# Attention scores and row maxima regrouped: 4 heads x 32 queries per matmul, keys in steps of 32

## The reference

```python
q = x @ wq_w.T + wq_b                    # x: (2, 1024, 256); 16 query heads of 16, 4 key heads of 16
k = x @ wk_w.T + wk_b
v = x @ wv_w.T + wv_b
q = _rope(q); k = _rope(k)               # the angle depends on the head alone
k = jnp.repeat(k, G, axis=1)             # G = 4 query heads share a key head
v = jnp.repeat(v, G, axis=1)
att = jnp.einsum('bhqd,bhkd->bhqk', q, k) / HD ** 0.5
att = jnp.where(mask[None, None], att, -jnp.inf)      # causal
att = jax.nn.softmax(att, axis=-1)
y = jnp.einsum('bhqk,bhkd->bhqd', att, v)
x = _layernorm(x + y @ cp_w.T + cp_b)
# then a feed-forward layer: one shared and 16 routed experts, 4 per token, and a second layernorm
```

## Time and profile before

| | |
|---|---|
| median of 3 runs | 551.21 us |
| span of the profiled execution, first to last instruction | 548.3 us |
| PE / DVE / ACT / POOL busy | 525.8 / 435.9 / 372.3 / 290.6 us |
| granted TensorE clock | 0.998 of full speed over the span |

### The profile page before, as it was taken

One profiled execution on the slowest core, in us unless ns is written; L12 is line 12 of the kernel. 1 busy time (PEld: TensorE's weight loads), 2 busy tenths in 40 slices (PEclk: granted clock), 3 DMA queues, 4 the chain that ended last, 5 costly groups with the idle time before them and its releaser, 6 DMA issues.

```text
span 548.3 us, 12215 instructions
## 1 busy us (share of the span) xinstructions
PE 525.8 (96%) x3796; PEld 359.4 (66%) x3796; DVE 435.9 (79%) x1126; ACT 372.3 (68%) x841; POOL 290.6 (53%) x336
## 2 busy tenths in 40 slices
PE   8999999999999899989999898899999999999885
PEld 4656444444554454534433387799999999999874
DVE  2388989899889899999992177987878788787685
ACT  2444777787888688968879566366766667667534
POOL 5121232555412777267978856477644454545292
PEclk9999999999999999999999999999999999999999
DMA  5934174400523811321042352378544443341495
GB/s 150 179 66 65 31 191 145 82 8 21 91 62 88 207 58 46 82 81 51 32 128 82 104 178 66 112 227 262 159 139 128 130 118 111 111 133 46 160 414 194
DMA packets 53710, 64.96 MB, mean 118 GB/s; under 512 B 8091, under 2 KB 47406, under 8 KB 53648
## 3 DMA queue, kind: packets, MB, share of 16 engines
q1 hardware_dynamic: 45968, 46.45, 31.4%
q0 software_dynamic: 7056, 17.60, 9.2%
q10 hardware_dynamic: 624, 0.13, 0.1%
HBM read 32.49 MB, written 25.62 MB: 106 GB/s over the span
## 4 chain that ended last, share of the span: by engine, by line
PE 75%; DVE 10%; POOL 6%; issue 3%; ACT 2%; DMA 2%; SPq 1%; POOLq 0%; DVEq 0%; ACTq 0%
PE psH L1705 13%; PE psS L1506 12%; PE psO L1491 11%; PE psT L1476 10%; PE psS L1568 4%; PE psX L1673 3%; PE psG L1716 3%; PE psS L1511 2%; PE psS L1592 2%; POOL xs_scratch L766 2%; PE psY L1733 2%; PE psY L1730 2%; PE psY L1729 2%; PE psY L1732 2%; PE psY L1731 2%
## 5 line engine op out<-in xcount | busy, mean ns | idle before, releaser
L885 ACT ACTIVATE prob<-psT 128x512 f32<-128x512 f32 (+3 forms) x384 | 167.3, 495 | 51.6 <-PE psT L1476 49.0
L1161 DVE TENSOR_REDUCE MX<-psS 128x1 f32<-128x512 f32 (+3 forms) x344 | 182.6, 595 | 9.1 <-PE psS L1511 3.9
L1506 PE MATMUL psS<-KS,QS 96*128 96x512 bf16 (+3 forms) x384 | 109.9, 328 | 4.4 <-DVE MX L1161 2.5
L839 POOL DMA_INDIRECT y_scratch<-ys,dst x79 | 76.9, 973 | 65.7 <-ACT ys L1040 50.8
L1476 PE MATMUL psT<-QS,KS 98*128 98x512 bf16 (+3 forms) x384 | 107.0, 328 | 0.9 <-ACT prob L885 0.4
L795 POOL TENSOR_SCALAR_AFFINE_SELECT prob<-prob 128x512 f32<-128x512 f32 x64 | 42.4, 665 | 91.8 <-ACT prob L885 91.6
L1491 PE MATMUL psO<-prob,V 128*32 128x512 f32 (+3 forms) x768 | 81.3, 498 | 1.2 <-POOL prob L795 1.2
L1705 PE MATMUL psH<-wU,xh 128*128 (+1 forms) x380 | 80.8, 334 | 0.5 <-DVE z L1313 0.4
L766 POOL DMA_INDIRECT xs_scratch<-x1row,slotu x64 | 65.4, 1022 | 26.9 <-issue 16.2
L1476 PEld LDWEIGHTS psT<-QS,KS 98*128 98x128 bf16 x384 | 33.7, 97 | 52.9 <-ACT prob L885 34.6
L1506 PEld LDWEIGHTS psS<-KS,QS 96*128 96x128 bf16 x384 | 37.1, 98 | 45.4 <-DVE MX L1161 22.5
(11 more groups left out here) (260 smaller groups left out, 1003.0 us busy)
## 6 DMA issues: line engine op xcount, KB each, us to landing
xs<-xs_scratch SPq DMA_DIRECT2D x80, 134.0 KB
y<-y_scratch SPq DMA_DIRECT2D x16, 512.0 KB, 10.2
QS<-qp SPq DMA_DIRECT2D x48, 128.0 KB, 4.5
wU_raw<-in_L_ffn_w_routed_dram SPq DMA_DIRECT2D x32, 176.0 KB, 2.9
xs_scratch<-padrow SPq DMA_DIRECT2D x1, 2144.0 KB
xs_scratch<-padrow SPq DMA_DIRECT2D x16, 134.0 KB
x1row<-in_L_attn_x_dram SPq DMA_DIRECT2D x4, 512.0 KB, 5.8
out_dram<-x1row SPq DMA_DIRECT2D x7, 256.0 KB, 2.6
```

The source lines that it names most:

```text
L839: nc.gpsimd.indirect_dma_start(y4_dram, bass.IndirectOffsetOnAxis(ap=dst[:, n % NSEL, t:t + 1], axis=0), ys[:, n % NYS, t, :], None, bound ...
L885: nc.scalar.activation(prob[:, step % NPROB, h, 0:HALF - c0], ps[:, 0:HALF - c0], ACT.Exp).then_inc(s_Tfree, 1)
L1161: found = nc.vector.tensor_reduce(out=MX[:, c0 // HALF, heads[0]:heads[-1] + 1, i - TH * q], in_=src, op=ALU.max, axis=AX_X)
L1506: last = mm(ps[:, e * dist:e * dist + cols], QS[0:ROWS, QAT[(k // 2) % NSLOT], g % 2 * G + h, (i - TH * q) * P:(i - TH * q + 1) * P], KS[b ...
```

## The change

The queries of a half are regrouped. The half's 512 queries are 16 blocks of 32; block p holds queries 32p to 32p+31. The columns of QS are written in a new order, query 32p + i in column 16 i + p, by reading the projection's input with a step of 32 columns. From this follow:

- `smax`: one matmul takes 4 heads x 32 queries of one block, whose columns lie 16 apart, as its 128 stationary columns. A block needs keys only up to its own end, (p+1) x 32 of the half. Two blocks with together 512 keys share a PSUM bank and one mask matmul, whose stationary matrix `spread_b` repeats a 32-row identity for the 4 heads; the mask has 32 columns per block. A q = 0 headgroup has 9 units with 16 score matmuls, 9 masks and 16 reduces, a q = 1 headgroup 16 more units of 512 keys.
- `mrow`: DVE's result, 128 partitions (4 heads x 32) by 16 blocks, already has the column order of QS, so SP sends it directly by two DMAs, each of 128 pieces of 16 bf16. Transpose and copy are gone, and M2 has two buffers.
- `st`: one matmul takes 4 heads x 128 queries (4 neighbouring columns, then 16 on), always 512 columns: 4, 3, 2 and 1 items on the diagonal. ACT's exponential writes 4 heads x 128. POOL clears the diagonal of the first chunk of a step and waits for that chunk alone; its pattern now steps through 4 blocks of 32.
- `evac` puts the queries back in order while it copies: it reads psO with a step of 4.
- ORDER is written anew (911 items for 1079), and the order of two projection splits is exchanged.

```diff
 def max_units(q):
-    if q:
-        return [(i, (h,), c, HALF, c0) for i in range(TH, TT) for h in range(G) for c0, c in ((0, HALF), (HALF, (i + 1) * P - HALF))]
-    units = [(0, (0, 1, 2, 3), P, P, 0)] + [(1, (h, h + 1), 2 * P, 2 * P, 0) for h in (0, 2)]
-    units += [(i, (h,), (i + 1) * P, HALF, 0) for i in (2, 3) for h in range(G)]
-    return units
+    near = [(NBLK - 1,)] + [(NBLK - 2 - i, i) for i in range(NBLK // 2 - 1)] + [(NBLK // 2 - 1,)]
+    return ([("far", p) for p in range(NBLK)] if q else []) + [("near",) + u for u in near]
+def segments(unit):
+    kind, *blocks = unit
+    if kind == "far":
+        return [(blocks[0], 0, HALF)]
+    return [(p, 0 if n == 0 else HALF - (p + 1) * QB, (p + 1) * QB) for n, p in enumerate(blocks)]
...
 ORDER = """
-aaaaaaaadadpaaldppdlpdaaaapalaaaaapaapamalpppaxxaaaxxaaxaalxxxaaxxvamaxxavxxxaaaxavaxaxpaxmaxaxaaxxaaxvxaaaxxaexpavmaaxx
+aaaaaaaadpdlaadapppldalaaaaaaaamaappaapapapxapaxdxwaxpaxaaxxaaavvaaxaamxlawxxpaxdaxvvxxaaalaexaxxvvxamaxxaxaaxvwvweaxaax
...
+        def heads_of(k, r0, r1):
+            g = HEADGROUPS[k][2]
+            return QS[r0:r1, QAT[(k // 2) % NSLOT], g % 2 * G:(g % 2 + 1) * G, :]
...
-                    sp.wait_ge(s_Tfree, T_NO[item])
-                    sp.dma_start(QS[ROWS:QROWS, QAT[(k // 2) % NSLOT], g % 2 * G:(g % 2 + 1) * G, :]
-                                 .rearrange("s h (i t) -> s (h i) t", t=P), MT[:, :]).then_inc(s_mrow, 16)
+                    sp.wait_ge(s_Sfree, S_NO[last_max(k)])
+                    for s in range(MROWS):
+                        sp.dma_start(heads_of(k, ROWS + s, ROWS + s + 1).rearrange("a h (i p) -> a (h i) p", p=NBLK),
+                                     M2[:, k % 2, s, :]).then_inc(s_mrow[k % 2], 16)
...
-                                            pattern=[[0, G], [1, P]], channel_multiplier=-1).then_inc(s_diag, 1)
+                                            pattern=[[0, G], [1, QB], [QB, G]], channel_multiplier=-1).then_inc(s_diag, 1)
...
-                    nc.scalar.activation(prob[:, step % NPROB, h, 0:HALF - c0], ps[:, 0:HALF - c0], ACT.Exp).then_inc(s_Tfree, 1)
+                    nc.scalar.activation(prob[:, step % NPROB, :, c * P:(c + 1) * P], ps.rearrange("p (h t) -> p h t", h=G),
+                                         ACT.Exp).then_inc(s_Tfree, 1)
...
-                    nc.scalar.copy(O[:, k % 2, :], psO[:, :]).then_inc(s_evac, 1)
+                    nc.scalar.copy(O[:, k % 2, :].rearrange("d (c p i) -> d c p i", c=TH, i=QB),
+                                   psO[:, :].rearrange("d (c i p) -> d c p i", c=TH, i=QB)).then_inc(s_evac, 1)
...
-                    found = nc.vector.tensor_reduce(out=MX[:, c0 // HALF, heads[0]:heads[-1] + 1, i - TH * q], in_=src,
-                                                    op=ALU.max, axis=AX_X)
+                    for p, at, cols in segments(unit):
+                        found = nc.vector.tensor_reduce(out=MX[:, int(q and unit[0] == "near"), p:p + 1], in_=ps[:, at:at + cols],
+                                                        op=ALU.max, axis=AX_X)
...
-                    mm(ps[:, 0:HALF - c0], KS[b][:, g, j * P:(j + 1) * P],
-                       QS[:, QAT[(k // 2) % NSLOT], g % 2 * G + h, c0:HALF], start=True, stop=True).then_inc(s_T, 1)
+                    mm(ps, KS[b][:, g, j * P:(j + 1) * P],
+                       heads_of(k, 0, QROWS).rearrange("r h (i p) -> r h i p", p=NBLK)[:, :, :, p1:p1 + P // QB],
+                       start=True, stop=True).then_inc(s_T, 1)
...
-                    for e, h in enumerate(heads):
-                        last = mm(ps[:, e * dist:e * dist + cols],
-                                  QS[0:ROWS, QAT[(k // 2) % NSLOT], g % 2 * G + h, (i - TH * q) * P:(i - TH * q + 1) * P],
-                                  KS[b][0:ROWS, g, c0:c0 + cols], start=True, stop=not masked)
-                        if masked:
-                            d = e * dist + cols - P
-                            last = mm(ps[:, d:d + P], ident_b[:, :], mask_b[:, :], start=False, stop=True)
+                    for p, at, cols in parts:
+                        last = mm(ps[:, at:at + cols], heads_of(k, 0, ROWS).rearrange("r h (i p) -> r (h i) p", p=NBLK)[:, :, p],
+                                  KS[b][0:ROWS, g, k0:k0 + cols], start=(at == 0), stop=not near)
+                    if near:
+                        d = [at + cols - QB for _, at, cols in parts]
+                        step = d[-1] - d[0]
...
+                        last = mm(to, spread_b[:, :], by, start=False, stop=True)
...
-                elif kind == "mrow":
-                    pe.wait_ge(s_Sfree, S_NO[last_max(item[1])])
-                    nc.tensor.transpose(ps[0:MROWS * G * TH, :].bitcast(BF16)[:, 0:P], M2[:, :, :].rearrange("p s r -> p (s r)"),
-                                        ident_b[:, :]).then_inc(s_T, 1)
...
-                        last = mm(ps[0:rows, 0:HALF], wT[:, k, :],
-                                  xT[:, k, half * HALF:(half + 1) * HALF], start=(k == 0), stop=(k == KC - 1))
+                        src = xT[:, k, half * HALF:(half + 1) * HALF]
+                        if m:
+                            src = src.rearrange("c (p i) -> c i p", i=QB)
+                        last = mm(ps[0:rows, 0:HALF], wT[:, k, :], src, start=(k == 0), stop=(k == KC - 1))
```

More of the change, by code:

```diff
@@ L45 @@
 NPROB = 3
+QB = P // G
+NBLK = HALF // QB
 assert NHALF * NKV == TT
@@ L173, in plan @@
         "v": [("pv", k, n) for k, n in STEPS], "n": [("norm", k) for k in range(NK)], "r": [],
-        "p": later_items(0) + first_items(1) + later_items(1), "x": [("st", k, n, h) for k, n in STEPS for h in range(G)],
+        "p": later_items(0) + first_items(1) + later_items(1), "x": [("st", k, n, c) for k, n in STEPS for c in range(chunks(k, n))],
         "w": [], "s": [], "o": [], "c": []}
@@ L184, in plan @@
             streams["c"] += [("scat", b, q, n) for n in range(TH * TOPK)]
-    streams["d"] = [("split",) + i[1:] for i in streams["a"] + streams["p"] if i[0] == "proj"]
+    projected = [i for i in streams["a"] + streams["p"] if i[0] == "proj"]
+    projected[2:4] = projected[3:1:-1]
+    streams["d"] = [("split",) + i[1:] for i in projected]
     for u, _ in weight_units():
@@ L189, in plan @@
         streams["o"] += [("wlow",) + u] if u[0] == "wB" else []
-    queues = {c: iter(items) for c, items in streams.items()}
+    return streams
+def plan():
+    queues = {c: iter(items) for c, items in item_streams().items()}
     return [next(queues[c]) for c in "".join(ORDER.split())]
@@ L234 @@
 SEL_NO = {item: n + 1 for n, item in enumerate(
-    i for i in SEQ if i[0] == "st" and i[3] == G - 1 and exp_steps(HEADGROUPS[i[1]][1])[i[2]][2])}
+    i for i in SEQ if i[0] == "st" and i[3] == 0 and exp_steps(HEADGROUPS[i[1]][1])[i[2]][2])}
 LASTCP = ("cp", B - 1, TT - 1)
@@ L443, in attention_moe @@
         s_qload = [sem(f"s_qload{i}") for i in range(NSLOT)]
-        s_mrow = sem("s_mrow")
+        s_mrow = [sem(f"s_mrow{i}") for i in range(2)]
         s_res = sem("s_res")
@@ L634, in run @@
                         last = 2 * (s - NSLOT) + 1
-                        sp.wait_ge(s_T, T_NO[("st", last, len(exp_steps(HEADGROUPS[last][1])) - 1, G - 1)])
+                        sp.wait_ge(s_T, T_NO[last_exp(last)])
                     if s:
@@ L725, in link @@
                 pool.wait_ge(s_pool, chain[0])
-            for m in (ident, ident_b, mask_b, padrow):
+            for m in (ident, ident_b, spread_b, mask_b, padrow):
                 nc.gpsimd.memset(m[:, :], 0.0).then_inc(s_const, 1)
@@ L1484, in run @@
                         pe.wait_ge(s_evac, k)
-                    st = ("st", k, n, G - 1)
                     if diag:
-                        pe.wait_ge(s_diag, SEL_NO[st])
-                    else:
-                        pe.wait_ge(s_Tfree, T_NO[st])
+                        pe.wait_ge(s_diag, SEL_NO[("st", k, n, 0)])
+                    if not diag or chunks(k, n) > 1:
+                        pe.wait_ge(s_Tfree, T_NO[("st", k, n, chunks(k, n) - 1)])
                     for h in range(G):
@@ L1503, in run @@
                         pe.wait_ge(s_qload[s % NSLOT], 16 * len(PAIRS) * (s // NSLOT + 1))
[L1504 to L1511 removed]
+                    near = unit[0] == "near"
+                    k0 = HALF if q and near else 0
+                    parts = segments(unit)
+                    for p, at, cols in parts:
[4 more added lines that the diff above has]
+                        step = d[-1] - d[0]
+                        to = ps[:, d[0]:d[0] + QB]
+                        if step:
+                            to = bass.AP(tensor=to.tensor, offset=to.offset, ap=[to.ap[0], (step, 2), (1, QB)])
+                        by = mask_b[:, :].unsqueeze(1).to_broadcast([P, 2, QB]) if step else mask_b[:, :]
+                        last = mm(to, spread_b[:, :], by, start=False, stop=True)
                     last.then_inc(s_S, 1)
```

79 lines of the change are left out of this document (38 added, 41 removed).

## The result

The changed kernel takes 584.62 us (median of 4 runs, 584.04 to 585.33) where the kernel before, on the same chip, takes 551.98 (four runs, 550.10 to 556.87): a ratio of 1.056, 95% interval 1.051 to 1.061. It is slower by 32.6 us; 538 was forecast, and the range ended at 556.

What follows compares the result with a forecast made beforehand. PE sets the pace with DVE close behind; -15.3 (DVE) + 0.3 + 0.6 (end) + 1 (selects) + 0.5 (evacuation) = -12.9 us takes the span from 548.3 to 535.4, so about 538 us measured; forecast 531 to 546, 8-in-10 range 528 to 556.

Steps and rivals of the forecast that it cites:

- POOL's select: Select in runs of 4 queries: 0.61 us as now, up to 0.5 more by an iota's 1.1; 1 us taken.
- elsewhere POOL is half idle: Outside the end, slower selects cost nothing; in the end 7 of them cost 0 to 3.5 us.
- I take nothing for all three: PE's stepped reads of QS as weights, QS in the scores and xT in the projections cost 0 us.
- the upper bound (13.7 us): Query projections reading xT with a step, at half rate: 13.7 us more on PE.
- rival 2: Steps cost PE: projections 13.7 and weights 11.5 us make PE decide, 559 us, slower; chance 0.12.
- One more DMA a headgroup; it mostly waits: SP's queue: one more DMA issued per headgroup, listed among the smaller edits with no cost taken.
- rival 3: Gain not handed on: row maxima in 32-byte pieces land 1 to 1.5 us later, 550 us; chance 0.10.
- PE's maxima: Near-block score matmuls and masks of a headgroup go from 3.11 to 2.16 us, 15.2 us over 16.
- The smaller saving decides: Ahead of the last maxima DVE's saving, 15.3 us, sets the gain; M2 of headgroup 15 ready near 275 us.
- PE's 19.5: PE's work ahead of the last maxima falls by 17 us plus 1.5 and 1.0 handed to the end.
- rival 1: PE and DVE both give more: DVE's idle shrinks, PE's 19.5 decides, 534 us, down to 529; chance 0.07.
- The end: From last M2 to last evacuation, POOL's scatters and selects set 22.5 us, 0.6 us longer than now.

Runs made afterwards that it cites:

- experiment 1: Changed kernel; exponentials read PSUM with the step and write prob in natural order, so POOL's select has runs of 128: 558.3 us, ratio 1.012.
- experiment 2: Kernel before; only the pattern of POOL's select is cut into runs of 4, same data and result: 576.61 us, ratio 1.045.
- experiment 7: Changed kernel with selects over runs of 128, projections reading xT without step, 2.1 MB padding transfer behind headgroup 3's row maxima: 536.99 us (0.970), again 538.41 (0.976).
- experiment 9: Kernel of experiment 7 plus filler matmuls of ones where TensorE paused in the first 43 us: 533.59 us, ratio 0.970, against 538.41 without.
- experiment 4: Kernel before; only the query projections read xT with a step of 32 columns, ScalarE and VectorE undo the order: 565.39 us, ratio 1.022.
- experiment 5: Changed kernel with selects over runs of 128 and query projections reading xT without a step, DMA order left alone: 545.61 us, ratio 0.986.

## Why the prediction was wrong, step by step

The forecast missed by 584.6 - 538 = 46.6 us, and the three edits together gave back 47.6. Three terms of the sum were wrong: POOL's select most of all, then the stepped projections, then the queue of SP.

**The step that failed: POOL's select.** The prediction bounded it by the iota, 1.1 us, took +1 us in all, and let "elsewhere POOL is half idle" hide the rest. That term measured 26.3 us (experiment 1) and 24.0 (experiment 2). Both halves of it were wrong. The iota was no bound for a select: 1.59 us lies above it; by (1591 - 656) / 512 the runs of 4 cost 1.8 ns an element on top of the 1.3 that it takes in any case. And a share of idle time says nothing about a latency that stands in an in-order queue. One place of the changed kernel shows how; POOL, ACT and PE:

```profile
199.57 0.97 POOL L794 DMA_INDIRECT xs_scratch<-x1row,slotu  x1 [0.30 <-issue]
200.55 1.49 POOL L817 TENSOR_TENSOR x1row<-x1row,cpb_b 128x256 f32<-128x256 f32 x1
202.01 4.65 POOL L823 TENSOR_SCALAR_AFFINE_SELECT prob<-prob 128x512 f32<-128x512 f32 x3
...
205.95 0.59 ACT L921 COPY O<-psO 128x512 f32<-128x512 f32 x1 [3.78 <-PE psO L1517]
...
200.81 0.39 PE L1502 MATMUL psT<-QS,KS 98*128 98x512 bf16 x1
203.63 0.64 PE L1517 MATMUL psO<-prob,V 128*32 128x256 f32 x8 [2.43 <-POOL prob L823]
205.18 0.65 PE L1517 MATMUL psO<-prob,V 128*32 128x128 f32 x8 [0.90 <-POOL prob L823]
205.76 0.65 PE L1534 MATMUL psS<-KS,QS 96*128 96x352 bf16 x2
206.20 0.26 PE L1543 MATMUL psS<-mask_b,spread_b 128*128 128x64 bf16 x1
```

The last selects of a headgroup come in a row, 1.55 us apart, behind POOL's other work; the products behind them take PE 0.6 us each, so PE stands at each, and everything in PE's order with it. The last two rows show the second price: two pieces of 352 and 160 columns take 206.20 - 205.76 = 0.44 us, where 512 columns took 0.22. Behind the pauses TensorE runs at 1.2 GHz; the stretch before them and the one with these rows (the third figure from the end is the granted clock):

```profile
200.00:202.50 2.50, 1.21 (x9) 0.66 (x7) 2.44 (x6) 2.17 (x5) 2.49 (x3) 1.00 0.79 222
...
205.00:207.50 2.50, 2.32 (x17) 1.53 (x18) 1.00 (x3) 0.62 (x2) 2.33 (x3) 0.50 1.17 132
```

The granted clock over the whole span says how much that is, for the changed kernel, and for the kernel of experiment 7:

```profile
core 0: 583.6 us, clock 0.962
```

```profile
core 0: 535.6 us, clock 0.982
```

With two levels, 0.038 below full speed is 0.038 / 0.5 x 583.6 = 44 us at 1.2 GHz; the kernel before, at 0.998, has 2. An estimate of what that costs is at most half of it, 22 us, less where PE stood anyway. It is no fourth loss beside the three: the gains of the edits make up the whole difference without it. The select's edit by itself (clock 0.981) brings the 44 us down to 0.019 / 0.5 x 557.6 = 21; the slow select by itself brings the kernel before (0.978 in experiment 2) up to 0.022 / 0.5 x 573.3 = 25. So of the select's 26.3 us the clock makes at most some 12, by the same estimate; the other 14 or more are left to PE's waits. That a pause of PE brings the clock down is shown directly by experiment 9, for the first 50 us; elsewhere it is read from the order of events.

**The stepped operands.** "I take nothing for all three" was right for the weights: their load went from 98 to 149 ns, and the score pieces of the maxima still start 0.22 us apart for 512 columns, with the load hidden. It was nearly right for the scores, 14 ns each instead of none. For the projections the upper bound (13.7 us) was what came, 14.1; the reason, that a float32 column has time to hide a slower read, was wrong. So was rival 2's own counter-argument that the first projections stand in a start that waits for loads anyway: 7 us were lost there (experiment 4). Rival 2, which had this mechanism, deserved more than 0.12, though its 559 us has no select in it. The Trainium skill (Advanced Engine Details and Errata, SBUF Cachelines) has full rate only with two hits on a line of 16 bytes; it gives no size for what a miss costs. The traces agree for the projections, which have one (1040 ns for 599), and for the load of the weights (149 for 98); by that rule the scores, with four, pay nothing, and there the measurement differs a little (395 for 381) and decides.

**SP's queue.** "One more DMA a headgroup; it mostly waits" looked at the wrong thing, and rival 3 too. The pieces of 32 bytes are harmless:

```profile
QS<-M SPq DMA_DIRECT2D x32, 4.0 KB, 2.0
```

2.0 us to landing is less than the 3.6 feared from the earlier trace rows. What counted was the place in the queue: ORDER moved a 2.1 MB transfer ahead of one of the sixteen hand-overs. It stood in the two ORDER strings and was not looked for. Moving it gave 5.5 us in the changed kernel and 8.6 on top of the other two edits; the runs of experiment 5 alone spread over 5.4 us, so that the two figures are not told apart.

**What held.** PE's maxima, here in the changed kernel's timeline at full clock:

```profile
121.51 0.18 PE L1543 MATMUL psS<-mask_b,spread_b 128*128 128x32 bf16 x1
121.54 0.39 PE L1502 MATMUL psT<-QS,KS 98*128 98x512 bf16 x1
121.77 0.38 PE L1534 MATMUL psS<-KS,QS 96*128 96x480 bf16 x2
122.00 0.19 PE L1543 MATMUL psS<-mask_b,spread_b 128*128 128x64 bf16 x1
```

A mask takes 0.03 us to the next start, the pieces of 480 and 32 columns 0.23, as costed. DVE's reduces fell from 182.6 us of busy time (344 of them) to 172.3 (384), the 10 us of the sum. The evacuation's step cost nothing (591 ns), less than the 0.5 taken. With the three places mended (experiment 7) the last M2 is ready at 275.1 us, forecast 275, the last evacuation starts at 298.8, forecast 299, and the time is 537 to 538, forecast 538.

**That agreement is partly luck.** "The smaller saving decides", DVE's 15.3 us, does not hold: with the fillers the last M2 is ready at 270.9 us, 19.2 earlier than in the kernel before. That is near PE's 19.5 and not DVE's 15.3, though the scores' step still costs 288 x 14 to 19 ns, 4.0 to 5.5 us; with this cost taken off, PE's terms give 14 to 15.5, and the 4 to 5 us beyond them are not explained. The stretches of experiment 7 point to PE as well: it is idle 3.3 of 242.8 us (4.4 of 261.5 before), DVE 18.4 (20.7 before). So PE seems to pace and DVE waits less than before, as rival 1 had it; no run slows one of the two alone in the mended kernel. In experiment 7 the low clock, most of it in the first 50 us, took back some 4 of the 19.2 us, which left 15.0, the size of the false bound.

**The end** came to 31.2 us for 22.5: seven selects of 1.6 us among the scatters, which the sum there had priced at 0.6 to 0.65, make some 7 of the 9 us, and the clock is 0.84. With short selects it is 23.7.

What stays open: why the clock still falls in experiments 7 and 9 for a few microseconds near 150 and 265 us, where no pause of PE stands out. All four falls begin within some 2 us behind a run of the router's 16 float32 matmuls of 16 columns (in experiment 7 from 149.70 to 151.75 us, with a granted clock of 0.79 and 0.53 in the stretches of 2.5 us from 150.0 and 152.5). But the same run at 220.80 us is followed by none, nor are the three in the kernel before, so that this is no explanation yet. Nor is it measured how the select's 26.3 us divide between wait and clock; there is only the bound above.

## What to carry to other kernels

When a layout is changed for one engine's sake, list every other reader of the tile with the length of its inner run, and price each by a test in which that alone is changed; PSUM readers on ScalarE and VectorE could undo the order here for nothing, where GpSimd and TensorE from SBUF could not. An engine that is half idle can still hold up the program: look at what stands behind its slowest instruction in the in-order queues, and at what the same engine does just before. And where the order is written anew, walk the DMA queue for large transfers that have come ahead of small ones that someone waits for.

## What the runs showed of the hardware that was not expected

- A select of GpSimd over 128 x 512 float32 takes 0.66 us with a pattern of inner runs of 128 and 1.60 with one of runs of 4, on the same contiguous data (experiments 1 and 2).
- TensorE reading float32 from SBUF with a step of 128 bytes takes twice the time from start to start (0.86 us for 0.43; 1040 ns for 599 in the group's mean); bf16 in runs of 8 bytes every 32 takes 4% more of the mean duration (395 for 381).
- Weights read with a step of 32 bytes load in 149 ns instead of 98, hidden behind a matmul of 512 columns.
- ScalarE and VectorE read PSUM with such steps at no cost: ScalarE's copy of a projection takes 686 to 688 ns either way and an exponential 606, VectorE's part of a projection 750 to 751.
- Fifteen filler matmuls in pauses of TensorE gave back 3 to 5 us (538.4 to 533.6 by the medians), by the clock that they kept up.
